# A four-layer graph network in one kernel: the gated unit's loop written out with each chunk's state, norm and transposes inside later chunks, and the last layer's spread, skip and bias placed differently

## The reference

```python
x = _layernorm(x + _L0_gnn_ref(x, adj, adj, ...), axis=-1)   # attention and two gated units
x = _layernorm(x + _L1_gnn_ref(x, adj, ...), axis=-1)        # adj @ (x W) / degree, then a linear layer
x = _layernorm(x + _L2_gnn_ref(x, adj, ...), axis=-1)        # masked softmax-like attention
x = _layernorm(x + _L3_gnn_ref(x, adj, ...), axis=-1)        # graph convolution, then a selective scan
# end of layer 0
edge_output = _gru_cell(node_support, h, ...)                # r, z = sigmoid(..), n = tanh(i_n + r * h_n)
node_output = _gru_cell(edge_support, h, ...)                # out = (1 - z) * n + z * h
return de[:, None] * edge_output + dn[:, None] * node_output
# layer 3
h = relu(adj @ x @ gcn_w + gcn_b); h = norm(h) * ln_g + ln_b
xc, z = split(h @ w_in); u = silu(conv(xc)); dt, B, C from u @ w_xp
state = exp(dt * A) * state + dt * B * u                     # 256 channels x 16 states, along the 2048 rows
y = (state @ C + u * D_skip) * silu(z); return y @ w_out
```

## Time and profile before

| | us |
|---|---|
| median of 3 runs | 918.31 |
| the three runs | 918.03, 918.31, 923.39 |
| the profiled execution, whole | 922.9 |
| its span in the profile | 921.1 |

### The profile page before, as it was taken

The page is one execution under the profiler, slowest core; times in us unless marked ns, Lnnn a source line. Parts: engine busy times, 40 slices in busy tenths (PEclk is TensorE's granted clock), DMA queues, the critical chain, the costliest instruction groups (busy, mean ns, idle before and its releaser), DMA issues. The chain is left out here.

```text
span 921.1 us, 11988 instructions
## 1 busy us (share of the span) xinstructions
PE 812.2 (88%) x4192; PEld 522.0 (57%) x4192; DVE 684.2 (74%) x976; ACT 516.1 (56%) x838; POOL 235.3 (26%) x135
## 2 busy tenths in 40 slices
PE   6999989999999999999589979989969889796664
PEld 6655538888888888864345559974322233331211
DVE  3986989999999999517752337863177889889997
ACT  2753537777777787535320127532566667766561
POOL 2000000000000000000020010001399879868992
PEclk8999998999999999999889989999879989897767
DMA  8689885220122021059300000000332615606310
GB/s 282 223 307 339 343 293 224 92 92 22 69 91 91 0 91 46 1 213 422 124 1 1 1 1 1 1 1 23 73 102 71 138 47 130 136 26 155 86 46 11
DMA packets 38958, 101.64 MB, mean 110 GB/s; under 512 B 6113, under 2 KB 11114, under 8 KB 32386
## 3 DMA queue, kind: packets, MB, share of 16 engines
q1 hardware_dynamic: 38354, 100.83, 33.1%
q10 hardware_dynamic: 560, 0.27, 0.1%
HBM read 75.60 MB, written 18.14 MB: 102 GB/s over the span
## 5 line engine op out<-in xcount | busy, mean ns | idle before, releaser
L1789 PE MATMUL PS<-big 128*128 128x256 f32 x768 | 194.6, 385 | 3.4 <-ACT big L1619 3.2
L221 PE MATMUL PS<-ident,big 128*128 128x128 f32 x1123 | 159.1, 282 | 41.2 <-ACT big L656 19.2
L221 PEld LDWEIGHTS PS<-ident,big 128*128 128x128 f32 x1123 | 137.6, 146 | 64.0 <-issue 39.3
L463 POOL TENSOR_TENSOR big<-big 128x1024 f32<-128x1024 f32 x64 | 149.6, 2354 | 14.0 <-DVE big L1359 9.4
L1789 PEld LDWEIGHTS PS<-big 128*128 128x128 f32 x768 | 133.7, 191 | 21.7 <-ACT big L1619 7.0
L1619 ACT ACTIVATE big<-PS 128x512 f32<-128x512 f32 x192 | 105.0, 598 | 58.8 <-PE PS L221 57.9
L1359 DVE TENSOR_TENSOR_SCAN big<-PS,stripes,big 128x512 f32<-128x512 f32 x96 | 116.6, 1263 | 4.7 <-ACT PS L722 2.4
L414 POOL MEMSET big<- 128x16 f32 x1 | 0.1, 125 | 462.6 <-DVE big L1168 462.6
L1988 DVE SCALAR_TENSOR_TENSOR big<-big,rz 128x2048 f32<-128x2048 f32 x48 | 112.7, 2350 | 0.9
L1966 DVE CUSTOM_DVE_ANT_0 big<-big 128x2048 f32<-128x2048 bf16 x48 | 109.7, 2289 | 0.1
L722 ACT ACTIVATE PS<-big,stripes 128x512 f32<-128x512 f32 x128 | 85.9, 685 | 34.5 <-DVE big L1359 34.1
(11 more groups left out here) (210 smaller groups left out, 1006.0 us busy)
## 6 DMA issues: line engine op xcount, KB each, us to landing
big<-in_adj SPq DMA_DIRECT2D x16, 2048.0 KB, 8.9
big<-at_dram SPq DMA_DIRECT2D x4, 4096.0 KB, 27.1
at_dram<-big SPq DMA_DIRECT2D x3, 4096.0 KB, 16.5
big<-b_dram SPq DMA_DIRECT2D x32, 256.0 KB, 4.3
big<-big SPq DMA_DIRECT2D x24, 256.0 KB, 4.0
big<-b_dram SPq DMA_DIRECT2D x36, 128.0 KB, 3.9
at_dram<-big SPq DMA_DIRECT2D x1, 3072.0 KB, 18.4
big<-e_dram SPq DMA_DIRECT2D x3, 1024.0 KB, 6.8
```

What stands on the lines that cost most here:

```text
L221: return nc.tensor.transpose(PS[:, bank, col:col + P], src, ident[:])
L463: nc.gpsimd.tensor_tensor(dbu[k % 3], du2[c % 2][:, 2 * (n % 2):2 * (n % 2) + 2, :], bb[group % 2][:, pair_of(k) % 2, :].unsqueeze(1).to_b ...
L1789: m = nc.tensor.matmul(PS[:, 4 + k // 3, 0:256], hw[:, jt, h, :], qt[v % 4][:, 256 * c:256 * c + 256], start=(h == 0 and jt == 0), stop=(h ...
```

## The change

In the gated unit the three loops are written out. The state of chunk c - 1 is transposed by TensorE within the second half of chunk c, into bank 3, and added to x by VectorE in that half; its statistics and scaling follow a chunk later. The transposes of x for quarter 0 stand in chunk 2's second half, those of quarter 1 behind the loop. H1 moves to another place. The adjacency product of chunk 0 takes four tiles after each quarter. In the last layer the spread that serves VectorE's next own step is issued ahead of the sum of the step before it; the skip product and the bias product of chunks 1 to 3 are replaced by ScalarE writing u * D_skip and the bias into PSUM, to which TensorE adds; h_fill of chunks 2 and 3 moves behind the output product.

```diff
-        H1, AHT = SC[:, 0:N], SC[:, N:2 * N]
+        H1, AHT = SC[:, 9 * CH:9 * CH + N], SC[:, N:2 * N]
...
+        def spread_after(k):
+            if on_pool(k):
+                return None
+            own = [i for i in range(k + 1, STEPS) if not on_pool(i)]
+            return own[0] if own and spreads(own[0]) else None
...
# loads (SyncE's queue)
+            sp.wait_ge(l2_xev, 4)
+            sp.wait_ge(w3_in, 16 * 10)
+            sp.dma_start(dgt[:], t["L3_gnn_gcn_b"].partition_broadcast(P)).then_inc(w3_in, 16)
             sp.wait_ge(x_ready, 12)
             sp.dma_start(cwb, t["L3_gnn_conv_w"].partition_broadcast(P)).then_inc(cw_in, 16)
...
# GpSimd: the ones column after the selection tables instead of before them
-            pool.wait_ge(x_ready, 4)
-            nc.gpsimd.memset(x2[:, :, P], 1.0).then_inc(ones_col, 1)
...
+            pool.wait_ge(l1_mm, 4)
+            nc.gpsimd.memset(x2[:, :, P], 1.0).then_inc(ones_col, 1)
...
# ScalarE, gated unit (squash is the old loop body)
+            for c in range(NCH):
                 for g in range(2):
+                    squash(c, g)
+                    if c >= 2 and g == 0:
+                        root(0, c - 2)
+                if c == 2:
+                    xt_copy(1, 0, 2)
+            xt_copy(1, 1, 2)
             root(0, 2)
+            for q in range(2):
+                evac(l1_h, q + 1, H1, q, 4 + q, l1_hev)
+            for q in range(2, 4):
+                if q == 3:
+                    root(0, 3)
+                xt_copy(1, q, q - 1)
                 evac(l1_h, q + 1, H1, q, 4 + q, l1_hev)
...
# ScalarE, last layer: a_copy and skip
                 act_copy(ahg, PS[:, bank, :]).then_inc(a_ev, 1)
+                if c:
+                    act.wait_ge(a_ev, 2 * c)
+                    act.wait_ge(w3_in, 16 * 11)
+                    act_copy(PS[:, bank, :].rearrange("p (s f) -> p s f", f=P),
+                             dgt[:].unsqueeze(1).to_broadcast([P, 4, P])).then_inc(a_ev, 1)
...
+            def skip(c):
+                act.wait_ge(y_done, c)
+                for b in range(DI):
+                    m = act_copy(PS[:, 2 + b, :], u[:, b, :], scale=dskip[:, b:b + 1])
+                m.then_inc(skip_mm, 1)
...
                     save_state(k)
+                if c and n == 0:
+                    skip(c)
                 if c < NCH - 2:
                     chunk_after(c + 2, n)
...
# TensorE, gated unit
+            def st_transpose(q):
+                pe.wait_ge(gru_out, 2 + 2 * (q + 1))
+                if q < NCH - 1:
+                    pe.wait_ge(tanh_out, 2 + 2 * (q + 1) + 1)
+                for b in range(4):
+                    m = transpose_into(3, b * P, nst[:, 4 * q + b, :])
+                m.then_inc(st_mm, 1)
+            def x_transpose(q, bank):
+                pe.wait_ge(x_ready, q + 1)
+                xt_fill(1, q, bank, X)
+            def gates(c, g):
...
+                if g == 0 and c == 3:
+                    pe.wait_ge(xt_ev, 5)
+                nc.tensor.matmul(PS[:, 4 * g + 2, :], wt[:, wi + 2, :], xs, start=True, stop=True)
+                if g == 1 and c:
+                    st_transpose(c - 1)
+                if g == 1 and c == 2:
+                    x_transpose(0, 2)
+                if g == 0 and c >= 2:
+                    pe.wait_ge(st_read, c - 1)
+                nc.tensor.matmul(PS[:, 4 * g + 3, :], wt[:, wh + 2, :], hx, start=True, stop=True).then_inc(gru_mm, 1)
...
+            x_transpose(1, 2)
+            pe.wait_ge(tanh_out, 2 + 2 * NCH)
+            for q in range(2):
                 features(q)
+            pe.wait_ge(st_read, 3)
+            st_transpose(3)
+            for q in range(4):
+                if q >= 2:
+                    x_transpose(q, q - 1)
+                    features(q)
+                pe.wait_ge(l1_hev, q + 1)
+                adjacency_product(hj, 0, 4 * q, 4 * q + 4, l1_mm)
...
# TensorE, last layer: bias product and skip product kept for chunk 0 alone
-                pe.wait_ge(a_ev, c + 1)
-                nc.tensor.matmul(PS[:, bank, :], ones_row, gcn_b.unsqueeze(1).to_broadcast([1, 4, P]), start=True, stop=False)
+                pe.wait_ge(a_ev, 2 * c + 1)
+                if c == 0:
+                    nc.tensor.matmul(PS[:, bank, :], ones_row, gcn_b.unsqueeze(1).to_broadcast([1, 4, P]), start=True,
+                                     stop=False)
...
                     if c:
-                        pe.wait_ge(y_done, c)
+                        pe.wait_ge(skip_mm, c + 1)
...
-                if n == 1:
+                if n == (1 if c == 1 else 2):
                     if c >= 2:
                         pe.wait_ge(zg_ready, 3 * (c - 1))
                     h_fill(c, 0)
-                elif n == 2:
+                if n == 2:
                     conv_part(c, 0, 0, range(0, 2))
...
+            spread(next(k for k in range(STEPS) if spreads(k)))
             for k in range(STEPS):
                 c, n = k // STATES, k % STATES
-                if spreads(k):
-                    spread(k)
-                if n == 1 and 0 < c < NCH - 1:
-                    next_chunk(c + 1, n)
                 for i in sums_at(k):
+                    after = spread_after(i)
+                    if after is not None:
+                        spread(after)
                     add_up(i)
-                if c < NCH - 1 and (n != 1 or c == 0):
-                    next_chunk(c + 1, n)
                 if c and n == 1:
                     pe.wait_ge(yg_ready, c)
+                    pe.wait_ge(h_ready, c + 2 if c < NCH - 1 else c + 1)
                     out_product(c - 1, 1, range(4), o_mm)
+                if c < NCH - 1:
+                    next_chunk(c + 1, n)
...
# VectorE, gated unit
+            for c in range(NCH):
+                to_tanh(c, 0)
+                if c >= 2:
+                    spread_of_x(c - 2)
+                mix(c, 0)
+                if c == 3:
+                    diagonal_back(0)
+                if c >= 2:
+                    scale_x(c - 2)
+                to_tanh(c, 1)
+                if c:
+                    add_state(c - 1)
+                if c == 3:
+                    diagonal_back(1)
+                mix(c, 1)
+            spread_of_x(2)
+            scale_x(2)
+            add_state(3)
+            spread_of_x(3)
+            scale_x(3)
+            for b in range(2, 4):
                 diagonal_back(b)
```

More of the change, by code:

```diff
@@ L520, in later_act, with squash @@
             act.sem_inc(tanh_out, 2)
-            with act.Fori(0, NCH) as c:
-                for g in range(2):
[L523 to L533, removed]
-            root(0, 2)
[L535 to L538, removed]
+            def squash(c, g):
+                act.wait_ge(gru_mm, c * 2 + g + 1)
+                act.wait_ge(gru_out, c * 2 + g + 1)
+                nc.scalar.activation(gate_r[g], PS[:, 4 * g, :], ACT.Sigmoid, bias=gbs[:, g, 0:1])
+                nc.scalar.activation(gate_z[g], PS[:, 4 * g + 1, :], ACT.Sigmoid, bias=gbs[:, g, 1:2]).then_inc(gate, 1)
+                act.wait_ge(tanh_in, c * 2 + g + 1)
+                nc.scalar.activation(gru_n[g], gru_t[g], ACT.Tanh, bias=gb[:, 2 * g, 2:3]).then_inc(tanh_out, 1)
+            for c in range(NCH):
+                for g in range(2):
+                    squash(c, g)
[4 more added lines that the diff above has]
+            xt_copy(1, 1, 2)
+            root(0, 2)
+            for q in range(2):
[4 more added lines that the diff above has]
+                xt_copy(1, q, q - 1)
                 evac(l1_h, q + 1, H1, q, 4 + q, l1_hev)
@@ L833, in later_pe @@
             pe.wait_ge(xt_ev, 4)
-            with pe.Fori(0, NCH) as c:
-                for g in range(2):
[L836 to L850, removed]
+            nst = ns[:].rearrange("p (t i) -> p t i", i=P)
+            def st_transpose(q):
[5 more added lines that the diff above has]
+                m.then_inc(st_mm, 1)
@@ new lines, in chain, with to_tanh @@
+            def chain(c, step, ins):
+                ins.then_inc(gru_step, 1)
+                dve.wait_ge(gru_step, c * 7 + step)
+            def to_tanh(c, g):
+                dve.wait_ge(gate, c * 2 + g + 1)
+                chain(c, 3 * g + 1, nc.vector.scalar_tensor_tensor(gru_t[g], PS[:, 4 * g + 3, :], gb[:, 2 * g + 1, 2:3],
+                                                                   gate_r[g], ALU.add, ALU.mult))
+                nc.vector.tensor_tensor(gru_t[g], PS[:, 4 * g + 2, :], gru_t[g], ALU.add).then_inc(tanh_in, 1)
@@ new lines, in mix @@
+            def mix(c, g):
+                dve.wait_ge(tanh_out, c * 2 + g + 3)
+                chain(c, 3 * g + 2, nc.vector.tensor_tensor(gru_t[g], XT[:, c * CH:(c + 1) * CH], gru_n[g], ALU.subtract))
+                chain(c, 3 * g + 3, nc.vector.tensor_tensor(gru_t[g], gru_t[g], gate_z[g], ALU.mult))
+                if g == 0:
```

(12 more changed lines are left out.)

78 lines of the change are left out of this document (30 added, 48 removed).

## The result

The changed kernel takes 932.29 us (median of 4 runs, 931.78 to 936.2), the kernel before beside it 919.23 (918.03 to 923.39): a ratio of 1.0128, 95% interval 1.0086 to 1.017. (The medians are 13.1 us apart, 1.42% of the lower one; a ratio here comes with its interval and is not the quotient of two medians.) The profiled execution has a span of 934.4 us against 921.1.

A forecast was written before the change was run, and what follows sets the result against it. No engine was full over the span; TensorE paced the gated unit, VectorE the last layer. Gated unit +5.4 and last layer +4.1 make +9.5 us on the 918.31 median: forecast 928, range 914 to 935.

The forecast's parts named there:

- both sums positive: The forecast case: gated unit +5.4 us and last layer +4.1 us both cost time; chance 0.48.
- the bound of 1%: Whole kernel: differences under 9.2 us can hardly be told from none; slower 0.42, within 0.50, faster 0.08.
- part 1: Gated unit to layer 1's product: new queue order makes TensorE wait, +5.4 us, bounds +2.5 to +8.5.
- the last layer: Earlier spreads gain 1.2 us twice, the skip on ScalarE costs 3.2, 2.6 and 0.7: +4.1, bounds -4 to +7.
- the two quarter chains: Layer 1's adjacency product: transpose-to-feature chains of quarters 2 and 3, 6.1 and 3.2 us; a third less gives +2.5.
- the lower clock in two quarters: Adjacency product, quarters 2 and 3: pieces take 5.46 us against 3.5, putting the gated unit's sum at +8.5.
- Table loads hidden: Gated unit, chunks 2 and 3: ScalarE's 1.28 us loads end before VectorE asks; rival that they show, 930 us, 0.04.
- Spreads, -1.2 in each of chunks 0 and 1: Last layer: earlier spreads mostly turn 15.7 us of weighing waits into decay waits; rival that all return, 908 us, 0.12.
- Skip, +3.2, +2.6, +0.7: Last layer, chunks 1, 2, 3: ScalarE's skip waits for the gated product and delays h_scale four us; costs as named.

The follow-up runs named there:

- spreads_only: The kernel before with one edit, each spread issued ahead of the sum of the step before it: 921.29 us, ratio 0.9993.
- after_again: The same changed kernel measured and profiled a second time beside the kernel before: 932.02 us, ratio 1.0112.
- last_only: The kernel before with the last layer's changes alone (spreads, bias and skip on ScalarE, later h_fill): 924.47 us, ratio 1.0023.
- skip_later: The changed kernel with the skip one step later in ScalarE's queue, behind h_scale: 923.53 us, ratio 1.0003.
- the two halves timed alone: The kernel before with only the gated-unit and layer 1 changes, 926.42 us (ratio 1.0027), and with only the last-layer changes, 924.47 us (ratio 1.0023).
- nostall: The changed kernel with the x transposes of quarter 0 one chunk later, in chunk 3's second half: 926.68 us, ratio 1.0071.
- tail: The changed kernel with quarters 2 and 3 transposed together after the first four product tiles, features after the second four, quarter 3's root ahead of the copies: 923.99 us, ratio 1.0021.

## Why the prediction was right, point by point

The forecast was +9.5 us on the profiled execution, or 928; it came out at +1.28% and, measured again, +1.12%, which is 10 to 12 us of 919 (by the medians 13.1 and 8.7 us). The likeliest case was the one that happened, both sums positive. Both ratios lie above the bound of 1%, a side to which I gave 0.42, less than the 0.50 for within 1%; their intervals reach down to 0.86 and 0.76%, so the side is not settled. In the first profile the stages give +13.3: 5.4 for part 1 as forecast, 6.3 for the last layer where I had 4.1, and 1.6 that the forecast does not have.

- *Gated unit, +5.4*: 5.2 to 5.4 in five profiles (81.0 to 81.2 less 75.7). The order of the queues was right almost to the step: scaling done 438.8 (forecast 439.4), VectorE's second half of chunk 3 at 456.01 (456.3), mixing ended 462.46 (463.0), layer 1's last features 490.43 (490.5). Two terms inside were off and cancelled: eight of the first tiles' matmuls did not run at the lower clock, so the piece from 464.53 took 7.1 instead of 9.0, and quarter 2 started at 477.32 instead of 480.3; there the lower clock struck, 6.60 instead of 3.5, which I had only in the bounds. That these cancel is luck, and the sum is better than its terms deserve. The bounds were also added up loosely: a third off the two quarter chains gives +2.3, not +2.5, and the lower clock in two quarters (twice 5.46 less 3.5) +9.3, not +8.5.
- *Table loads hidden*: the sigmoid at 454.26 starts when the load of 452.97 ends, and VectorE comes at 456.01, so nothing is late by it. The Trainium skill ("ScalarE: Activation LUTs", What ACT_TABLE_LOAD costs) gives about 2.66 us a switch with a drain; the trace does not show the drain (the root ends at 452.95, the load starts at 452.97 and ends as the sigmoid starts), and the stage is 5.4 longer, not 7.1. Here the measurement decides.
- *Spreads, -1.2 in each of chunks 0 and 1*: mis-sized. What stands is that the wait is converted, shown by spreads_only at the row where I expected it. The gain is 0.3 to 0.8 in chunk 0 (81.4 and 80.9 against 81.7), 0.3 in chunk 1, and in the time nothing that shows. The waits for decays grew by 17.9 us, more than the 15.7 that went.
- *Skip, +3.2, +2.6, +0.7*: with the 1.2 of chunk 1 taken off, 5.3 for the three chunks; measured 7.1 in the changed kernel, 5.8 in after_again, 5.1 in last_only. The mechanism is the one forecast: the convolution starts 13.1 after the gated product (forecast 13.0, before 10.05), h_scale behind ScalarE's wait, and skip_later, which takes only that wait away, gains the loss back. What the term for chunks 1 and 2 left out is that decays are queued behind the same wait: the scan at 747.01 stands 1.87 for one, and skip_later has 14.4 us of decay waits where the changed kernel has 20.3.
- *Outside the change*: +1.6 in the layers between, from a stretch at 1.2 GHz that the second profile lacks.

What stays open: the two halves timed alone add up to 0.5% (their stages to about +10 us), the whole is 1.1 to 1.3%. The profiles show unedited stages that come out 2 to 6 us apart from one execution to another with the granted clock, enough to cover it, but I did not show that a half meets the better one more often than the whole.

## What to carry to other kernels

Moving a small step into a busy engine's queue is priced by the wait it brings, not by its length: two copies, 1.3 us together, cost 6.7 us over three chunks ahead of h_scale and won 2.6 behind it. Work that is woven into a loop should be consumed one iteration later than the first moment it could be, or the loop waits for it (nostall), and a group of short dependent steps should be put side by side so that each hides the other's hand-over (tail). Before a wait is attacked, read what the next instruction of the same engine is going to wait for: here the 15.7 us of the weighing were the scans' own wait in another name.

## What the hardware showed that I had not expected

- The granted clock moves stages that no edit touched: layers 1 and 2 take between 166.3 us (nostall, mean clock 0.98 in the stage) and 172.1 (spreads_only, 0.94). In spreads_only the 32 matmuls shown above, 3.81 us in the kernel before, took 6.71. The same kernel's chunk 0 took 80.9 and 78.9; these are the windows of its first tenth in the first and the second profile, 0.62 and full speed:

```profile
661.40:669.49 8.09, 8.09 (x14) 2.73 (x12) 1.38 (x2) 4.35 (x8) 4.88 (x3) 0.62 0.24 66
```

```profile
658.93:667.02 8.09, 8.09 (x20) 3.11 (x18) 2.08 (x3) 7.41 (x14) 5.34 (x4) 1.00 0.26 66
```

- A gap of a few microseconds was paid twice here: the product of eight matmuls after the 3.37 us wait took 6.60 and 5.37 in two kernels, at a mean granted clock of 0.55 and 0.68, and 3.60 at 1.00 where no wait stood ahead of it (tail, 469.86). After the 2.77 us wait in chunk 2 two matmuls took 1.92, at 0.50, instead of 1.02.
- A table load of 1.28 us is followed at once by its activation (452.97 and 454.26), and starts 0.02 us after the activation ahead of it ends (452.95).
